# Quantised feed-forward: the inverse block scale is made on ScalarE, behind the Silu of the next sequence, instead of on VectorE

## The reference, cut to what matters

```
def _quantize_mx(x, ebits, mfrac, emax_elem, max_norm):
    xb = x.reshape(shp[:-1] + (shp[-1] // BLOCK, BLOCK))
    amax = jnp.max(jnp.abs(xb), axis=-1, keepdims=True)
    sexp = jnp.floor(jnp.log2(jnp.where(amax == 0, 1.0, amax))) - emax_elem
    scale = jnp.exp2(sexp)
    q = _quantize_elem(xb / scale, ebits, mfrac, max_norm) * scale
...
gate = _mx_linear(x, w_gate)
up = _mx_linear(x, w_up)
inter = jax.nn.silu(gate) * up
return _mx_linear(inter, w_down)
```

## Time and profile before

| what | value |
|---|---|
| median of 3 runs | 792.35 us (791.91 to 794.6) |
| the profiled execution's own time | 793.81 us |
| its span, first to last instruction | 791.9 us |
| mean granted TensorE clock | 0.985 of full speed |
| PE busy | 737.5 us, 93% |
| DVE busy | 591.6 us, 75% |
| POOL busy | 565.6 us, 71% |
| ACT busy | 403.6 us, 51% |

### The profile page before, as it was taken

The page is one execution under the profiler, slowest core; times in us unless marked ns, Lnnn a source line. Parts: engine busy times, 40 slices in busy tenths (PEclk is TensorE's granted clock), DMA queues, the critical chain, the costliest instruction groups (busy, mean ns, idle before and its releaser), DMA issues.

```text
span 791.9 us, 14989 instructions
## 1 busy us (share of the span) xinstructions
PE 737.5 (93%) x4872; PEld 537.3 (68%) x4872; DVE 591.6 (75%) x1090; ACT 403.6 (51%) x1069; POOL 565.6 (71%) x588
## 2 busy tenths in 40 slices
PE   3999999988999999799999999999999999787886
PEld 2655555447888888666878777777777777654554
DVE  5889888958777769776566676776678676748996
ACT  1678788723323333335545554556564455554464
POOL 5667777426776767476566888887888888926995
PEclk9999999979999999999999999999999999998999
DMA  9300000022001110231300000000000000000101
GB/s 253 131 1 0 0 0 1 2 88 89 21 21 28 32 60 1 95 103 62 101 1 1 2 2 1 1 1 1 1 2 1 1 1 1 2 1 0 34 33 42
DMA packets 8764, 24.14 MB, mean 30 GB/s; under 512 B 1711, under 2 KB 5167, under 8 KB 8087
## 3 DMA queue, kind: packets, MB, share of 16 engines
q1 hardware_dynamic: 8154, 23.28, 8.9%
q10 hardware_dynamic: 549, 0.08, 0.1%
HBM read 21.26 MB, written 2.10 MB: 29 GB/s over the span
## 4 chain that ended last, share of the span: by engine, by line
PE 42%; DVE 7%; issue 4%; ACT 3%; POOL 2%; DVEq 0%; POOLq 0%; ACTq 0%
PE ps L1413 16%; PE ps L1460 4%; PE ps L1478 4%; PE ps L1427 4%; PE ps L1445 3%; PE ps L1430 3%; PE ps L1492 3%; DVE f_h L2125 2%; DVE ps L2137 2%; PE ps L1324 2%; POOL q L1748 1%; PE ps L2037 1%; ACT p L1568 1%; PE ps L1997 0%; ACT l_y L1558 0%
## 5 line engine op out<-in xcount | busy, mean ns | idle before, releaser
L1748 POOL TENSOR_TENSOR q<-turned 64x512 f32<-64x512 f32 x128 | 168.1, 1313 | 24.3 <-DVE turned L1672 11.4
L1413 PE MATMUL ps<-l_yt,a 128*128 128x512 f32 x576 | 144.1, 400 | 4.0 <-DVE a L1626 2.3
L1413 PEld LDWEIGHTS ps<-l_yt,a 128*128 128x128 f32 x576 | 105.1, 189 | 28.9 <-DVE a L1626 2.9
L1735 POOL TENSOR_TENSOR p<-p,l_inverse 128x512 f32<-128x512 f32 x64 | 66.5, 1042 | 65.4 <-DVE l_inverse L1694 64.4
L1672 DVE TENSOR_TENSOR turned<-ps,rope 128x1024 f32<-128x1024 f32 x64 | 78.0, 1219 | 40.6 <-PE ps L1413 36.3
L881 PE MATMUL ps<-yt_experts,wsplit 128*128 (+1 forms) x384 | 97.4, 403 | 0.1
L468 DVE TENSOR_REDUCE negmax<-ps 128x4 f32<-128x512 f32 x128 | 85.1, 685 | 15.0 <-PE ps L291 13.9
L1568 ACT ACTIVATE p<-ps,l_negmax 128x128 f32<-128x128 f32 x256 | 90.1, 389 | 4.9 <-DVE l_negmax L1663 4.9
L881 PEld LDWEIGHTS ps<-yt_experts,wsplit 128*128 128x128 f32 x384 | 71.6, 193 | 14.5 <-DVE inner L1036 0.3
L1585 ACT ACTIVATE qs<-ps 128x512 f32<-128x512 f32 x32 | 19.1, 597 | 105.9 <-PE ps L1430 105.9
L384 ACT ACTIVATE pt<-ps 128x512 f32<-128x512 f32 x128 | 69.8, 599 | 5.5 <-PE ps L313 3.8
(11 more groups left out here) (229 smaller groups left out, 1567.6 us busy)
## 6 DMA issues: line engine op xcount, KB each, us to landing
wide<-in_wide SPq DMA_DIRECT2D x8, 768.0 KB, 4.3
mx_raw<-in_mx SPq DMA_DIRECT2D x8, 384.0 KB, 3.1
x<-in_x SPq DMA_DIRECT2D x4, 512.0 KB, 8.7
ctx_t<-in_ctx_t SPq DMA_DIRECT2D x1, 2048.0 KB, 7.9
out<-x SPq DMA_DIRECT2D x16, 128.0 KB, 1.7
narrow<-in_narrow SPq DMA_DIRECT2D x8, 192.0 KB, 4.1
ktraw<-in_ctx_rows SPq DMA_DIRECT2D x1, 1248.0 KB
wraw<-in_gate SPq DMA_DIRECT2D x1, 1024.0 KB, 18.4
```

Source lines behind the costliest of these rows:

```text
L1413: out = pe.matmul(tile_bank(n, k), a[i][:, pa, kin, k * 128:(k + 1) * 128], yt[j % 2][:, py, kin, :, :].rearrange("p b s -> p (b s)"), sta ...
L1735: pool.tensor_tensor(p[:, head, :, :], p[:, head, :, :], spread(inverse[:, head, :], 2, S), ALU.mult).then_inc(normed[head], 1)
L1748: t = pool.tensor_tensor(out[rows[(head + half) % 2], head, :], turned[rows[head], half, :], turned[rows[head], 2 + half, :], ALU.add)
```

## The change

The third step of `scales_of_h` leaves DVE (`H_STEPS` falls from 3 to 2). ACT makes `hinverse` instead, from `hscale`, with one ACTIVATE Copy on the integer bits, scale -1 and bias INVERSE x 2^23, and raises a semaphore of its own, `h_inverted`, for which POOL's `h8` now waits. On ACT the inverse of sequence n - 1 stands in `body(n)` directly behind silu(n); that of sequence 0 behind silu(1).

```
-    H_STEPS, INVERSE = 3, 250
+    H_STEPS, INVERSE = 2, 250
...
             if inside(n, B):
                 silu(n)
+            if n >= 2 and inside(n - 1, B):
+                invert_scale(n - 1, (place - 1) % 4)
...
+        def invert_scale(n, place):
+
+            act.wait_ge(h_step, H_STEPS * (n + 1))
+            wait(act, h8_made, n - 1)
+            act.activation(hinverse[place % 2][:, :].bitcast(U32), hscale[place][:, :].bitcast(U32), ACT.Copy,
+                           bias=float(INVERSE << 23), scale=-1.0).then_inc(h_inverted, 1)
...
         silu(1)
+        invert_scale(0, 0)
         keep_context(END)
...
             then(2, dve.tensor_scalar(bits, hmax[par].bitcast(U32), EXPONENT, None, ALU.bitwise_and))
-            then(3, dve.tensor_scalar(hinverse[par][:, :].bitcast(U32), bits, -1.0, float(INVERSE << 23),
-                                      ALU.mult, ALU.add))
...
             if inside(n, B):
-                pool.wait_ge(h_step, H_STEPS * (n + 1))
+                pool.wait_ge(h_inverted, n + 1)
```

More of the change, by code:

```diff
@@ L1953, in feed_forward @@
         sem(n) for n in ("f_h_step", "f_h8_made", "f_hc_made", "f_hq_made", "f_hq_turned", "f_hq_kept"))
-    late_made = sem("f_late_made")
+    late_made, h_inverted = sem("f_late_made"), sem("f_h_inverted")
     down_made, x_made, bounded = sem("f_down_made"), sem("f_x_made"), sem("f_bounded")
```

## The result

The changed kernel has a median of 788.99 us (787.64 to 791.22, 10 runs) against 793.76 us before (791.91 to 795.22, 10 runs). The medians lie 4.8 us apart; the ratio of the means is 0.9947, with a 95% interval of 0.9933 to 0.9961: faster by 0.53%, about 4.2 us. Two later comparisons, on two different chips, gave 0.996 (0.9944 to 0.9976) and 0.9971 (0.9956 to 0.9986), that is 3.2 and 2.3 us. The span of the profiled execution fell from 791.9 to 787.0 us.

The account below looks back on a forecast made before the run. DVE was taken as the bound (4.09 us a round), POOL (3.75) and an 8.18 us detour close behind. Of 1.80 us saved by combine 9, POOL's `hq` 13 kept 1.57: 1.6 off 792.35 gives 790.7, range 789.0 to 793.0.

Parts of the forecast that it names:

- POOL becomes the bound: Whole layer: POOL takes over from DVE as the bound, 1.2 to 2.1 us off, 790.2 to 791.2; chance 0.56.
- DVE stays the bound: Rival, whole layer: POOL's late starts are made up, 2.9 us off, 789.4, or 788.7 without the waits; chance 0.16.
- DVE's saving up to combine 9: Combine 2 to combine 9: seven removals give 2.09, a wait for silu(5) costs 0.29; combine 9 starts 1.80 earlier.
- The detour: Combine 9 to 11 through PE and ACT, 8.18 us: DVE waits some 0.4 for silu(11), two removals bring nothing.
- `h8` of sequence 10: On POOL: it starts at 759.95 instead of 760.16, so 0.2 us is left of 1.80.
- POOL by then is full: POOL before `h8` of sequence 10: seven instructions from 746.8, behind silu(8), take 13.1 us and end at 759.95.
- POOL's own pace from there: From `h8` of sequence 10 to `hq` 13: ten POOL instructions take 18.75 us, ending at 778.7; gain 1.57.
- The end: Behind `hq` 13: the layer's end follows POOL through PE and ACT, then the last halves; 1.6 us earlier.
- The later of both is 1.6 earlier: Layer's end: sequence 14's `hq` on DVE ends 1.9 us earlier, POOL's `hq` 13 gains 1.57; the later sets 1.6.
- the port's rule takes nothing from the sum: Shared DVE and POOL port: gapless POOL does not slow combine, reduction and clip, with one SBUF input each; cost nothing.
- nothing: Rival, whole layer: ACT's lateness costs POOL about as much as DVE gives; time within 0.7 of 792.35; chance 0.19.
- the ring closes: Rival: the inverse puts ACT into POOL's loop, about 7.2 us against 7.5; slower, +2.5 to 794.9; chance 0.09.

Follow-up runs that it names:

- the second profile after: Changed kernel run again unchanged, as a control against the kernel before: 789.88 us, ratio 0.996; 71.59 us from combine 2 to the end.
- the second and the third profile of before: Kernel before run again unchanged, twice, as controls: ratio 0.9999 for the second, 793.80 us for the third.
- the kernel with the PSUM result: Changed kernel, but DVE keeps its third step and writes an unread spare result to PSUM; ScalarE still makes the real inverse: 792.66 us, ratio 0.9981 to before.
- the inverse of 10 first: Changed kernel with the inverse of sequence 10 ahead of silu(11) on ScalarE, not behind it: 791.12 us, ratio 0.9974 to before.
- the doubled Copy: Changed kernel, but ScalarE makes each inverse twice, the first time into a spare tile: 791.5 us, ratio 0.9962 to before.
- the single piece: Changed kernel, but POOL makes `h8` of sequence 15 in one piece instead of two: 789.81 us, ratio 0.9953 to before.

## Why the prediction was right, and where it was off

The direction was right, and the measured median of 788.99 lies, rounded, on the lower end of the range, 789.0. That the change would stay within 0.3% (0.67) did not come true: 0.53% in the first comparison, 0.4% and 0.29% in the later ones. The case that was put first, "POOL becomes the bound", is what happened, but the sizes of its terms were off: it gave 1.2 to 2.1 us, and the layer gained 2.6 to 2.9.

That the number fell into the range is in part luck. The sum starts from a median of 792.35, and the kernel before had 793.76 this time; the measured ratio on 792.35 would be 788.15 (an estimate), below the range. And the rival "DVE stays the bound", with 2.9 us, was nearer to the layer's gain than the forecast's 1.6. By the number alone one would have taken the wrong case for the true one; only POOL's rows and the kernels with more and less work on POOL tell them apart.

1. *DVE's saving up to combine 9*: right. 33.58 us after combine 2 was forecast; 33.61 where TensorE ran at half clock near 727 us, 33.31 and 33.33 where not.
2. *The detour*: right. silu(11) delays combine 11 by 0.33, against 0.4, and two removals bring nothing. It ended at 41.73 after combine 2 in the second profile after; 41.71 was forecast.
3. *`h8` of sequence 10*: mis-sized by 0.3 to 0.6. The step "POOL by then is full" held that silu(8) would be late and start POOL's row of seven instructions at 746.8. silu(8) was late in the profile of before because TensorE ran at half clock near 741 us: it ended 29.37 us after combine 2 there, and 27.87 in the second and the third profile of before, which lack that stretch. None of the three profiles after has it. In the second of them POOL was free at 41.24 us after combine 2, not at 42.25, and idled until silu(11) let the inverse go. That is 0.2 of the difference; the hand-over behind silu(11), 0.2 instead of 0.35, is nearly 0.15, and the full clock near 727 us in the other two profiles is 0.3. Where the stretch near 741 us is there, in the kernel with the PSUM result, silu(8) ended at 29.47 and POOL did wait for it:

```profile
746.42 1.91 POOL L2249 TENSOR_TENSOR f_h<-f_h,f_hinverse 128x1024 fp8e4<-128x1024 f32 x1 [1.35 <-ACT f_hinverse L2099]
```

4. *POOL's own pace from there*: right to the hundredth, 18.75 us for ten instructions (757.37 to 776.12). Five steps of 0.25 more added 1.28, and 0.2 less on each of the `h8` took POOL's gapless run away again and 0.69 off the layer; both show it was POOL.
5. *The end*: mis-sized by 0.7. The step "The later of both is 1.6 earlier" took the two chains of the end as tied before. DVE's was last by 0.7 us, as the chain in the profile of before says, in which `scale_back` and the halves stand and hqt(14) does not:

```profile
781.88 0.06 DVE f_hq L2186
...
783.66 1.28 DVE f_hc L2201 x2
...
785.04 1.05 DVE f_hq L2193
```

Counted from combine 2, DVE's `scale_back` ended 3.3 to 3.6 us earlier and the end of `hq` 13 only 2.0 to 2.2, so the end also got rid of the difference. About 0.3 of it the forecast had in its own terms, `scale_back` 1.9 us earlier where POOL was 1.6, and put at nothing: POOL's two pieces no longer start 0.3 behind `hq` 13. The rest, 0.3 to 0.4, is the port, of which `scale_back` got hold between POOL's pieces: where it did not, with the inverse of 10 first, the end took 11.28 us, not 10.9. The forecast had no term for this and said that the port's rule takes nothing from the sum.

Together 1.57 + 0.3 to 0.6 + 0.7 = 2.6 to 2.9 us, which is the table. The comparisons of whole runs gave 4.2, 3.2 and 2.3 us, with intervals of 1.1 to 1.3 either way. The two later ones take in the layer's gain; the first starts at 3.1 us, a little above it, and what the rest is stays open. Whether the change makes stretches at half clock a little rarer is not settled either: the mean granted clock was 0.987 to 0.988 in the runs of before and 0.989 to 0.992 in those after, but each kernel's own stretches vary.

Of the rivals, "DVE stays the bound" is ruled out behind sequence 10 by the extra work on POOL, "nothing" by all three comparisons, and "the ring closes" by the doubled Copy, which cost 0.14 us. The prediction also said that the removed step would have been stretched in every round by a POOL without gaps. With the step put back POOL had gaps again, and it was four rounds of sixteen.

## What to carry to other kernels

When a step of 0.2 us leaves the engine that sets the pace, ask how far the next engine is behind, per round, and stop counting there: here POOL was 0.34 us a round behind DVE, 0.12 after the change, and a single hand-over that came 1 us late used up the slack for the rest of the layer. A step that is queued behind a long one on another engine is late exactly where that engine is; look for those rounds in the profile of before, not at a typical one. And before adding up the end of a kernel, note which of its chains is last and by how much, since a change may shorten one and free the other.

## What the runs showed of the hardware

- A VectorE step of 0.18 us took 1.2 to 1.8 us in the four rounds of sixteen in which it began while a POOL instruction ran, and 0.20 in all rounds with its result in PSUM. In the kernel before, where POOL had a gap in most rounds, one in sixteen showed it (0.73).
- Who goes first can turn on a fraction of a microsecond. `scale_back` has two inputs in SBUF. Where it started 0.7 us behind POOL's first piece, it got in between the two pieces and took 1.45 us; where it started 1.0 behind, with the inverse of 10 first, it ended behind both and took 2.12. Behind the single piece it took 2.29, and with only one input in SBUF 1.22.
- TensorE's half clock for some 3 us came and went between executions of the same kernel. Ahead of combine 2 it followed the same 2.0 us of idling or did not, and cost 1.6 us; near 727 us it cost the changed kernel 0.3; near 741 us it cost the kernel before nothing, since its three profiles agree within 0.05 with and without it.
- An ACTIVATE Copy of 128x32 on integers takes 0.21 to 0.24 us (0.2 was forecast from 256 and 1024 columns), and where the next one on ScalarE has nothing to wait for, it starts 0.11 to 0.14 behind its start.
